# A two-direction state-space block in fp32: new instruction lists, a pipelined prologue and a convolution in four pieces

## The reference

```
xn  = layernorm(x)
xz  = xn @ in_proj_w.T                       # 256 channels x, 256 channels z
for each direction:                          # forward, and the reversed sequence
    u      = silu(conv4(x) + b)              # causal, 4 taps, per channel
    x_dbl  = xproj_w @ u                     # 8 rows for delta, 16 for B, 16 for C
    delta  = softplus(dtproj_w @ x_dbl[:8] + dt_bias)
    h[t]   = exp(delta*A) * h[t-1] + delta*B*u        # 256 channels x 16 states
    y      = sum_n h*C + D*u ;  y *= silu(z)
attn = (y_f + y_b) @ out_proj_w.T
xh = xn @ H ; s = max|xh| / 7 ; xq = clip(round(xh/s), -8, 7) * s
out = x + attn + xq @ ternary(w).T
```

## Time and profile before

| what | value |
|---|---|
| median of 3 runs (lowest, highest) | 984.36 us (981.34, 984.86) |
| profiled execution: its own time, its span | 989.38 us, 987.6 us |
| mean granted clock of PE | 0.875 of full speed |
| busy: PE, DVE, ACT, POOL | 802.9 (81%), 787.0 (80%), 780.7 (79%), 788.1 us (80%) |
| the chain that ended last, by engine | POOL 33%, issue 32%, ACT 13%, PE 11%, DVE 7% |
| DMA | 72.44 MB, mean 73 GB/s |

### The profile page before, as it was taken

One profiled execution on the slowest core, in us unless ns is written; L12 is line 12 of the kernel. 1 busy time (PEld: TensorE's weight loads), 2 busy tenths in 40 slices (PEclk: granted clock), 3 DMA queues, 4 the chain that ended last, 5 costly groups with the idle time before them and its releaser, 6 DMA issues.

```text
span 987.6 us, 13840 instructions
## 1 busy us (share of the span) xinstructions
PE 802.9 (81%) x3873; PEld 381.5 (39%) x3873; DVE 787.0 (80%) x795; ACT 780.7 (79%) x1452; POOL 788.1 (80%) x493
## 2 busy tenths in 40 slices
PE   2478887979888897888889797897978889797974
PEld 1134434343443434333353434434343343434352
DVE  2248887988888888888789887888978887988982
ACT  2469896988959887798869889698887988699950
POOL 1038978997899887898789977989879897798994
PEclk9677998899998989889879989889898898898796
DMA  3070607051160605215070421607043150704300
GB/s 86 11 162 29 135 4 182 3 123 41 57 136 3 159 3 124 68 53 107 3 170 24 115 44 39 154 3 159 3 104 88 33 129 3 169 15 99 61 22 11
DMA packets 50841, 72.44 MB, mean 73 GB/s; under 512 B 6128, under 2 KB 19328, under 8 KB 50816
## 3 DMA queue, kind: packets, MB, share of 16 engines
q1 hardware_dynamic: 50384, 71.87, 31.3%
q10 hardware_dynamic: 432, 0.26, 0.1%
HBM read 60.58 MB, written 11.53 MB: 73 GB/s over the span
## 4 chain that ended last, share of the span: by engine, by line
POOL 33%; issue 32%; ACT 13%; PE 11%; DVE 7%; SPq 1%; DMA 1%; POOLq 1%; DVEq 0%; ACTq 0%
POOL hst L612 22%; ACT da L370 5%; POOL dbx_t L622 5%; DVE hst L512 4%; PE pb L744 3%; ACT dbx_t L359 3%; POOL t_log L628 3%; PE b_ps L827 2%; PE b_ps L824 2%; POOL xn L674 2%; DVE b_ps L500 1%; PE pb L751 1%; PE y L841 1%; DMA rep<-d_scr 1%; PE pb L771 1%
## 5 line engine op out<-in xcount | busy, mean ns | idle before, releaser
L612 POOL TENSOR_TENSOR hst<-hst,c_rep 128x1024 f32<-128x1024 f32 x256 | 601.4, 2365 | 132.2 <-DVE hst L512 128.4
L512 DVE TENSOR_TENSOR_SCAN hst<-da,b_ps 128x512 f32<-128x512 f32 x512 | 589.5, 1203 | 82.1 <-ACT da L370 43.4
L827 PE MATMUL b_ps<-ident,dbx_t 128*128 128x128 f32 x1536 | 241.9, 298 | 127.3 <-DVE hst L512 120.1
L370 ACT ACTIVATE da<-rep,neg_a 128x511 f32<-128x511 f32 x512 | 335.6, 709 | 6.4 <-DMA rep<-d_scr 6.3
L827 PEld LDWEIGHTS b_ps<-ident,dbx_t 128*128 128x128 f32 x1536 | 178.2, 150 | 277.5 <-DVE hst L512 230.1
L359 ACT ACTIVATE dbx_t<-du_t,b_t 128x256 f32<-128x256 f32 x576 | 248.1, 495 | 2.9 <-PE b_ps L827 2.9
L841 PE MATMUL y<-hst,sum_sel 128*32 128x512 f32 x1024 | 166.6, 730 | 0.0
L744 PE MATMUL pb<-xnt,conv_wt 128*128 128x512 f32 x256 | 120.7, 616 | 0.7 <-ACT xnt L291 0.7
L824 PE MATMUL b_ps<-t_log,spread_sel 32*128 32x512 f32 x256 | 89.3, 698 | 10.6 <-DVE hst L512 10.6
L500 DVE TENSOR_TENSOR b_ps<-b_ps,b_rep 128x1024 f32<-128x1024 f32 x64 | 78.1, 1220 | 21.6 <-PE b_ps L824 21.6
L622 POOL TENSOR_TENSOR dbx_t<-du_t,b_t 128x1024 f32<-128x1024 f32 x48 | 91.2, 1901 | 2.7 <-ACT du_t L342 2.7
(11 more groups left out here) (90 smaller groups left out, 598.5 us busy)
## 6 DMA issues: line engine op xcount, KB each, us to landing
rep<-d_scr SPq DMA_DIRECT2D x128, 256.0 KB, 9.3
c_rep<-bc_scr SPq DMA_DIRECT2D x64, 256.0 KB, 5.0
d_scr<-t_pos SPq DMA_DIRECT2D x16, 512.0 KB, 3.0
b_rep<-bc_scr SPq DMA_DIRECT2D x64, 64.0 KB, 2.4
x_ln<-x SPq DMA_DIRECT2D x8, 256.0 KB, 3.2
x_res<-x SPq DMA_DIRECT2D x8, 256.0 KB, 2.9
out<-x_res SPq DMA_DIRECT2D x8, 256.0 KB, 9.5
conv_wt<-conv_w SPq DMA_DIRECT2D x2, 512.0 KB, 5.9
```

The costliest lines, as they stand in the source:

```text
L370: nc.scalar.activation(da[s % 2][:, j, 1:L], rep[d][h][:, j, 1:L], ACT.Exp, scale=neg_a[:, d, h, j, q:q + 1]).then_inc(decay_done, 1)
L512: nc.vector.tensor_tensor_scan(hst[s % RING][:, j, :], da[s % 2][:, j, :], b_ps[:, j, :], 0.0, ALU.mult, ALU.add).then_inc(scan_done, 1)
L612: nc.gpsimd.tensor_tensor(hst[s % RING][:, two, :], hst[s % RING][:, two, :], c_rep[d][:, q:q + 1, :].broadcast_to([P, 2, L]), ALU.mult).t ...
L827: ins = tr(b_ps[:, j, P * c:P * (c + 1)], dbx_t[(NX * d + q - 1) % 2][:, c, NJ * h + j, :, :].rearrange("p r e -> p (r e)"), ident[:, :])
```

## The change

Six things change; the lists of ACT and PE are written anew around them.

- Prologue: the layer norm and the first convolution stand ahead of the waits for the small weights. The first softplus, its DVE steps, the store of delta, the loads of `rep` and `make_du` are done in halves (`first_softplus`, `first_delta`, `first_du`), and `load_bc` is issued before the store of delta. The `spread_sel` products of slot 0 stand ahead of the convolution of unit 1.
- Step projections: the weights of `x_proj` stand twice side by side (128 columns instead of 64), so that `xdbl` has its rows on partitions 0 to 63 and again on 64 to 127. `steps(h)` uses rows 64*h on, and both stand together at the end of slot 1.
- Skip products: both stand in `sum_states` of slot 2, which PE reaches in its slot 3, instead of with slots 0 and 1.
- Convolution: four pieces of two taps, at the end of slot 6, in the middle and at the end of slot 7 and in the middle of slot 0, instead of two pieces of four taps.
- Quantization: `clip` and `rescale` go from POOL to DVE, right behind `quantize` in slot 6.
- ACT's list: `keep_xnt`, `keep_dut`, `normalize`, `keep_longer`, `z_sigmoid`, `u_sigmoid`, `inputs_t` and others stand later or earlier by up to a slot.

```diff
+            store_bc(0, 0)
+            load_bc(0, 0)
+            sp.wait_ge(first_delta, 1)
+            sp.dma_start(d_scr[0][0], t_pos[:, 0, :]).then_inc(first_stored, DMA)
+            sp.wait_ge(first_stored, DMA)
+            load_delta(0, 0)
+            sp.wait_ge(delta_ready, 1)
+            sp.dma_start(d_scr[0][1], t_pos[:, 1, :]).then_inc(delta_stored, DMA)
+            sp.wait_ge(delta_stored, DMA)
+            load_delta(0, 1)
...
-            spread(0, 0)
...
-                nc.scalar.activation(xdbl[d][0:XC, :], pb[0:XC, 1, :], ACT.Copy).then_inc(xdbl_ready, 1)
+                nc.scalar.activation(xdbl[d][:, :], pb[:, 1, :], ACT.Copy).then_inc(xdbl_ready, 1)
...
+            def first_softplus():
+                act.wait_ge(u_ready, 2)
+                act.wait_ge(dt_filled, 1)
+                nc.scalar.activation(t_exp[:, 0, :], pb[:, 0, :], ACT.Abs, bias=col[:, 0, 1, 0:1]).then_inc(sp_step, 1)
+                nc.scalar.activation(t_pos[:, 0, :], pb[:, 0, :], ACT.Relu, bias=col[:, 0, 1, 0:1]).then_inc(sp_step, 1)
+                act.wait_ge(sp_step, 2)
+                nc.scalar.activation(t_exp[:, 0, :], t_exp[:, 0, :], ACT.Exp, scale=-1.0).then_inc(first_step, 1)
+                act.wait_ge(first_step, 1)
+                nc.scalar.activation(pb[:, 0, :], t_exp[:, 0, :], ACT.Copy, bias=1.0).then_inc(first_step, 1)
...
+                nc.scalar.activation(pb[:, 1, :], t_exp[:, 1, :], ACT.Copy, bias=1.0).then_inc(sp_step, 1)
+                act.wait_ge(first_step, 2)
+                nc.scalar.activation(t_log[:, 0, :], pb[:, 0, :], ACT.Ln).then_inc(first_step, 1)
+                act.wait_ge(sp_step, 6)
+                nc.scalar.activation(t_log[:, 1, :], pb[:, 1, :], ACT.Ln).then_inc(log_ready, 1)
...
-            act.wait_ge(w_loaded, DMA * W_LOADS)
-            nc.scalar.activation(neg_a[:, :, :, :, :], neg_a[:, :, :, :, :], ACT.Exp).then_inc(a_exp, 1)
             log_var(0)
             guess_rstd(0)
             normalize(0)
             keep_xnt(0)
+            act.wait_ge(w_loaded, DMA * W_LOADS)
+            nc.scalar.activation(neg_a[:, :, :, :, :], neg_a[:, :, :, :, :], ACT.Exp).then_inc(a_exp, 1)
...
+            first_softplus()
...
-            inputs_t(0, 0, 1, 1)
...
+                    if s == 0:
+                        if d == 0 and not first(b):
+                            keep_dut(d, U, 1)
+                        inputs_t(d, U, 1, 1)
+                    if s == 1:
+                        inputs_t(d, U, 1, 3)
+                        if nxt:
+                            u_sigmoid(e, V, 1)
...
+                    if s == 0:
+                        inputs_t(d, U, 1, 2)
+                        if nxt:
+                            u_sigmoid(e, V, 0)
...
-                wait(dve, sum_done, SLOTS * (V - 2) + NH)
+                wait(dve, sum_done, SLOTS * (V - 2) + SKIP_AT)
...
+                    ins = nc.vector.tensor_scalar(pb[:, 0, at], pb[:, 0, at], qinv[:, c:c + 1], ROUND, ALU.mult, ALU.add)
+                ins.then_inc(xq_step, 1)
+                dve.wait_ge(xq_step, 2 * b + 1)
+                nc.vector.tensor_scalar(pb[:, 0, :], pb[:, 0, :], ROUND, Q_POS, ALU.subtract, ALU.min).then_inc(xq_step, 1)
+                dve.wait_ge(xq_step, 2 * b + 2)
+                for c in range(NC):
+                    ins = nc.vector.tensor_scalar(xq[:, c, :], pb[:, 0, P * c:P * (c + 1)], -Q_NEG, qscale[:, c:c + 1], ALU.max, ALU.mult)
+                ins.then_inc(xq_ready, 1)
...
-                    if s == 7 and d == 1:
-                        had_free(b)
...
-                    if s == 7 and d == 1:
-                        clip(b)
-                        clipped(b)
...
-                    if s == 7 and d == 1:
-                        rescale(b)
...
-                    ins = mm(pb[0:XC, 1, :], xproj[d][:, h, :], u[d][:, h, :], start=h == 0, stop=h == NH - 1)
+                    ins = mm(pb[:, 1, :], xproj[d][:, h, :, :].rearrange("p r c -> p (r c)"), u[d][:, h, :], start=h == 0, stop=h == NH - 1)
...
-                mm(pb[:, h, :], dtw[d][0:XC, P * h:P * (h + 1)], xdbl[d][0:XC, :], start=True, stop=True).then_inc(dt_filled, 1)
+                mm(pb[:, h, :], dtw[d][XC * h:XC * (h + 1), P * h:P * (h + 1)], xdbl[d][XC * h:XC * (h + 1), :], start=True, stop=True).then_inc(dt_filled, 1)
...
-                if q == 0:
-                    if d == 0:
-                        wait(pe, y_read, 2 * b - 1 + h)
+                if q == 0 and d == 0:
+                    wait(pe, y_read, 2 * b - 1 + h)
+                if s == SKIP_AT - 1:
                     pe.wait_ge(u_ready, 2 * (2 * b + d) + 2)
-                    mm(y[:, h, :], skip[:, d, h, :], u[d][:, h, step], start=d == 0, stop=False, skip_group_check=True)
+                    for n in range(NH):
+                        mm(y[:, n, :], skip[:, d, n, :], u[d][:, n, step], start=False, stop=False, skip_group_check=True)
                 pe.wait_ge(prod_done, 2 * S + 2)
                 for j in range(NJ):
                     ins = mm(y[CB * j:CB * (j + 1), h, :], sum_sel[:, :], hst[s % RING][:, j, step],
-                             start=False, stop=d == 1 and q == NQ - 1, skip_group_check=True)
+                             start=d == 0 and q == 0, stop=d == 1 and q == NQ - 1, skip_group_check=True)
                 ins.then_inc(sum_done, 1)
...
             pe.wait_ge(conv_loaded, DMA * 5)
             pe.wait_ge(zeroed, 8)
             transpose_xn(0, xn_ready, 1)
+            pe.wait_ge(weights_ready, 2)
+            pe.wait_ge(xnt_ready, 1)
+            conv(0, 0, 0, range(TAPS), xnt_ready, 1)
+            conv(0, 0, 1, range(TAPS), xnt_ready, 1)
             pe.wait_ge(fw_ready, 1)
-            tr(pb[:, 1, 0:DM], ft, ident[:, :]).then_inc(fwt_filled, 1)
+            tr(y[:, 0, 0:DM], ft, ident[:, :]).then_inc(fwt_filled, 1)
             pe.wait_ge(w_loaded, DMA * W_LOADS)
             pe.wait_ge(weights_ready, 5)
-            pe.wait_ge(xnt_ready, 1)
-            conv(0, 0, 0, range(TAPS), fwt_read, 1)
-            conv(0, 0, 1, range(TAPS), xnt_ready, 1)
             x_proj(0, 0)
-            b_transposed(0, 0, u_ready, 2)
+            steps(0, 0, xdbl_ready, 1)
             steps(0, 1, xdbl_ready, 1)
-            steps(0, 0, bt_ready, 1)
+            for c in range(NC):
+                ins = mm(y[:, 1, NS * c:NS * (c + 1)], xdbl[0][0:XC, P * c:P * (c + 1)], ident[0:XC, DR:DR + NS], start=True, stop=True)
+            ins.then_inc(bt_filled, 1)
+            pe.wait_ge(first_du, 1)
+            copies(0, 0, 0)
+            copies(0, 0, 1)
             du_transposed(0, 0, delta_ready, 1)
             du_transposed(0, 1, delta_ready, 1)
             conv(1, 1, 0, range(TAPS), dut_ready, 1)
             conv(1, 1, 1, range(TAPS), dut_ready, 2)
-            inputs(0, 0, 0, 0)
-            inputs(0, 0, 0, 1)
+            pe.wait_ge(fwt_read, 1)
+            pe.wait_ge(bt_ready, 1)
...
-                        steps(e, 1, xdbl_ready, V + 1)
...
                     if s == 7 and not last(b):
-                        if d == 0:
-                            conv(d, U + 2, 1, range(TAPS), dut_ready, 2 * V + 2)
-                        else:
-                            conv(d, U + 2, 0, range(TAPS), dut_ready, 2 * V + 1)
+                        conv(d, U + 2, 0, (2, 3), dut_ready, 2 * V + 1)
+                    if s == 0 and nxt and not (first(b) and d == 0):
+                        conv(e, V, 1, (2, 3), dut_ready, 2 * U + 2)
...
                     if s == 1 and nxt:
+                        steps(e, 1, xdbl_ready, V + 1)
                         steps(e, 0, bt_ready, V + 1)
...
                     if s == 6 and nxt:
                         if d == 1:
-                            du_transposed(V, 1, had_read, b + 1)
-                        elif not last(b):
+                            du_transposed(V, 1, xq_ready, b + 1)
+                    if s == 6 and not last(b):
+                        if d == 0:
                             pe.wait_ge(xnt_ready, b + 2)
-                            conv(d, U + 2, 0, range(TAPS), dut_ready, 2 * V + 1)
-                    if s == 7 and d == 1 and not last(b):
-                        conv(d, U + 2, 1, range(TAPS), dut_ready, 2 * V + 2)
+                        conv(d, U + 2, 0, (0, 1), dut_ready, 2 * V + 1)
+                    if s == 7 and not last(b):
+                        conv(d, U + 2, 1, (0, 1), dut_ready, 2 * V + 2)
```

169 lines of the change are left out of this document (93 added, 76 removed).

## The result

| | before | after |
|---|---|---|
| median (lowest, highest) of 4 runs | 984.61 us (981.34, 990.67) | 1000.19 us (997.53, 1000.61) |
| profiled execution: its own time, span | 989.38, 987.6 us | 1000.26, 998.1 us |
| mean granted clock of PE | 0.875 | 0.88 |
| busy: PE, DVE, ACT, POOL | 802.9, 787.0, 780.7, 788.1 us | 777.3, 801.4, 781.4, 750.2 us |

The ratio is 1.017 (95% interval 1.0135 to 1.0203): 1.7% slower. Forecast was 953 with a range of 932 to 973. The measured 1000.2 lies far outside and on the other side.

What follows compares the result with a forecast made beforehand. No engine was taken as the bound: four queues hold one another up, with DVE's scan chain to follow. -9.5 - 4.4 - 17.5 = -31.4 took the profiled 989.4 to 958.0; the median, 5.0 less, gave 953, range 932 to 973.

Steps and rivals of the forecast that it cites:

- Prologue: At the start: slot 1's first scan at 63.3 instead of 72.78 us, -9.5 us, bounds -6 and -13.
- End: Behind the last scans: `clip` and `rescale` on DVE let the last sums begin at about 972.3, -4.4 us, bounds -3 and -5.
- Quantization: Between the scans of slot 6: uncovered extra DVE work, +1.9 us a batch, bounds +1 and +2.5.
- slot 7 of direction 1: DVE's 2.34 us wait for decays goes, but PE is late instead: net 0 a batch, bounds -2.3 and +1.
- the last piece of the convolution in slot 0: Slot 0 of direction 0: it ends 2.4 us later and `make_u` waits, +2.2 us a batch, bounds 0 and +3.
- Slot 3 of direction 0: Skip products no longer precede the transposes, so DVE's 2.41 us wait goes: -2.2 us a batch, bounds -2.4 and 0.
- Slots 4 to 7: In direction 0: DVE's decay waits of 1.28, 1.48 and 0.98 us go, -3.5 us a batch, bounds -4.3 and -1.
- direction 1: 1.86 us in slot 3 goes, `u_sigmoid` costs 1.0 in slot 0: -0.9 us a batch, bounds -2.5 and +1.
- The sum: The six steady terms add to -2.5 us a batch, times 7 = -17.5 us.
- Rival (c): PE becomes the bound through its clock, convolution pieces run slow ahead of `spread_sel` products: +3.7 a batch, 996 us; chance 0.07.
- DVE's waits for decays: Sign of being right: these waits fall to at most a third of 6.9 us a period.
- the wait ahead of `u` in slot 0: Sign of being right: a new DVE wait for `t_exp` in slot 0 of direction 0, about 2 us.

Runs made afterwards that it cites:

- the two versions that differ in it: Changed kernel with two-piece convolution, first step projection in mid slot 1, `clip` and `rescale` on POOL: 960.1 us; these two on DVE in last batch only: 955.8 us.
- three parts: Undone singly in the changed kernel: convolution in two pieces, 979.7 us; first step projection in mid slot 1, 979.0; `clip` and `rescale` on POOL, 983.1.
- the fourth: The kernel before with one unused addition of 128x1024 on DVE behind each quantization: ratio 1.023 (1.013 to 1.033).
- a third: The changed kernel with four zero-weight products on PE ahead of the second transposes of slot 3 in each unit and slot 6 in direction 1: 1000.7 us.

## Why the prediction was wrong

- **Prologue** (forecast -9.5): right in kind and size, -8.8 in the trace. First decays came at 50.97 instead of 51.4, in part by luck: the convolution began at 15.47 instead of 14.3 and the store at 42.28 instead of 41, and the store and the loads took 2.0 and 6.7 us instead of 2.9 and 7.5.
- **End** (-4.4): right. -4.4 to the last sums and -5.3 to the last gate in the trace, -4.2 between the medians of the two versions that differ in it.
- **Quantization** (+1.9), **slot 7 of direction 1** (0) and **the last piece of the convolution in slot 0** (+2.2): right in place and size, +1.9, -0.3 and +2.1. I had found the new waits and still forecast a gain.
- **Slot 3 of direction 0** (-2.2): the step that failed, measured +0.8. The skip products did go, and DVE's wait of 2.41 us for the transposes with them: the slot's scan came 2.0 earlier against the step before it. But the next step, `log1p`, gained nothing by that. The logarithm had been ready at 548.58, 0.1 us before DVE came for it, so a wait of the same length stood hidden behind the 2.41, and I didn't look for it. On top of this I treated the grouped step projections as 1.1 us of PE time saved. They were also moved behind the second transposes of slot 2, and of this I priced nothing: ACT waits 2.33 us for them, and the logarithm ends 0.8 us later still (42.1 us behind the reciprocal instead of 37.6, where `u` is 3.7 later). DVE waits 2.69 for it: +2.8 at `log1p`, 2.0 of it the hidden wait and 0.8 the later logarithm. With the grouping undone `log1p` comes 1.3 us earlier, counted from `u`, which is 0.5 better than in the kernel before. That is what was left of the 2.2.
- **Slots 4 to 7** (-3.5): right in kind, measured -2.3; in **direction 1** (-0.9) the `u` wait was +1.8 instead of 1.0, and of the gain of 1.86 in slot 3 nothing came, since the scan there now waits 1.98 for decays: together +1.3. This too is the grouping: with it undone the 1.98 is gone. Undoing the grouping alone gave 979.0, 3.4 us a period, of which some 1.1 is the wait for the logarithm and most of the rest that for decays.
- **The sum.** These measured sizes give +3.4 a period. But the sum itself was the wrong tool: with only one of three parts undone, whichever it was, the kernel fell to the period of before. Terms of 1 to 2 us, each near right, don't say what a loop does that pays 21 us or 1.5 us for the same 1.22.
- **Rival (c)** (slower, 996): near in the result, and half right in its reason. Its pieces do cost (+10 alone). But it looked for them as DVE waiting for `b_ps` at a clock under 0.85, behind 4.8 us of idle PE. The clock was 0.88 and that idle time 3.17 us (519.03). The wait for transposes all but vanished. The one for the `spread_sel` products did grow, but with the pieces undone it is no smaller (27.2 us against 26.5 in all), and with the quantization on POOL it is 16.6. The pieces cost through tanh and `u`. What the clock costs isn't told by its mean: the changed kernel has 0.89 in its period at 119.5 us, the kernel before 0.88 at 116.0.

Signs that I had named: DVE's waits for decays are 2.7 us in the period, against at most 2.3; the wait ahead of `u` in slot 0 came with 2.06.

Shown: the ends, the price of the pieces, the worth of the new ACT list with the later skip products, that the loss isn't additive, and that in one kernel more work on PE alone takes 1% off, with periods that follow the clock. Open: why the changed kernel holds 119.4 us at a clock of 0.88 and of 0.907 alike, while kernels with one late step fewer hold 116.05 at 0.88. One of its late steps does fall on a slow stretch, the projections at 546.77 us:

```profile
546.60:550.60 4.00, 4.00 (x17) 0.79 (x16) 4.00 (x6) 1.98 (x4) 3.76 (x10) 0.57 0.00 0
```

The clock is 0.57 in these 4 us, and the projections take 1.75 us where they took 1.13 in the prologue. What of the loss is the step's place in the list and what its clock wasn't separated. Nor is it known why the values 112.6, 116.05 and 119.4 come back in different kernels, while others have periods between them.

## What to carry to other kernels

When a step is grouped with another to save time on its engine, price first who waits for the one that now comes later; the saving was 1.1 us and the wait 2.3. Before counting a wait as a gain, look when the next input behind it is ready: here it was ready 0.1 us before it was used, so a wait of 2.4 us that went away mostly came back under another name. Where four engines are some 80% busy in a lockstep loop, don't add up terms of 1 or 2 us: measure slack instead, by adding a known amount of useless work at the place and looking at what it costs; read from the trace how long that work takes in each kernel, here 1.22 us in three and 2.21 in the fourth. Undo each part of a bundle by itself before judging the bundle: this one held some 26 us of gain (982 to 956) under three parts that took all of it and more.

## What the hardware showed that was not expected

- The same program text ran its equal periods at 116.6 and 121.4 us in turn, with only the granted clock (0.88, 0.83) and what hangs on it differing, in a turn that repeats to 0.15 us.
- Useless products on PE made one kernel 1% faster and made another's periods nearly equal (112.6 us), while a third didn't change.
- The same addition on DVE took 1.22 us in three kernels and 2.21 in one, where POOL's product ran beside it.
- A row-tiled pair of projections ran side by side without a price that the trace shows. In the prologue both products (each counted as two instructions) took

```profile
31.89 1.13 PE L811 MATMUL pb<-xdbl,dtw 64*128 64x512 f32 x4 [0.69 <-ACT xdbl L338]
```

that is 1.13 us together. In the kernel before, one such product took 1.10 (536.26 us, at the high clock).
